# A graph kernel whose last three tiles of table rows are fetched one row at a time by the sync engine, with TensorE's turn put in another order

## The chip, the cores and the metric

The kernel runs on one core of a Trainium2 chip. A core has five engines that run side by side and meet only at semaphores: TensorE (PE), VectorE (DVE), ScalarE (ACT), GpSimd (POOL) and SyncE (SP), which here only issues DMA transfers. The metric is the device time of one launch in microseconds, as the median of several runs. One further execution was recorded by the profiler.

## The reference

Two graph layers over 3,125 nodes and 53,125 edges sorted by target, 128 features, all float32. Only the second one matters here:

```python
def sage_conv(x, src, dst, Wl, bl, Wr, n):      # layer 0, three of these with relu between
    agg = segment_sum(x[src], dst) / max(count, 1)
    return agg @ Wl.T + bl + x @ Wr.T

x = x + L0(relu(layernorm(x)), edges)
h = relu(layernorm(x))
messages = mlp(h[src] + edge_attr, We1, be1, We2, be2)   # gelu between the two products
aggregated = segment_sum(messages, dst)
x = x + mlp((1 + eps) * h + aggregated, Wu1, bu1, Wu2, bu2)
```

The kernel computes `h @ We1 + be1` once for each node and keeps it in HBM as `table` (3,125 rows of 512 bytes). For each edge it needs the row of its source node, added to `edge_attr @ We1`.

## The kernel before

The launch has a first part (adjacency counts and the three layers of L0, up to about 427 us), and then the **edge stage**, which the change touches. The edge stage walks over 416 tiles of 128 edges, in 105 groups `g` of 4 tiles (group 103 has three tiles, 412 to 414, and group 104 has one, 415). Each engine runs its own loop over turns `g`, written out by hand; what one engine hands to another is counted in a semaphore.

- **TensorE**, turn `g`: `mix(g + 2)` multiplies the edge attributes of a group by `We1` into one of three PSUM banks (`z_ready`); it waits for the edge load and for `pre_ready` of the group that had the bank. `take_sources` (line 1383) multiplies selection matrices for a picked group; `flip` (line 1392) transposes a picked group; `aggregate(g - 1)` (line 1425) adds the messages of a group to their nodes. The nodes come in seven chunks `c`; when the last group of a chunk is in, `node_mix`, `node_up` and `node_down` (lines 1400 to 1412) do the node MLP, with a turn for each set by `node_due`. Chunk 5 ends with group 100, chunk 6 with group 104.
- **GpSimd** fetches the source rows of a group from `table` by one indirect DMA for each tile (line 653) into a ring of six groups, `rows`. 15 of the 105 groups are "picked" (3, 10, 17, ..., 101): their rows come from TensorE's selections instead and are not gathered. That leaves 356 gathers.
- **VectorE**, turn `g`: the selection matrices of the picked groups (`select_sources`, line 945), the one-hot matrix of a group's targets (`window_onehots`, line 917), and then `pre = z + rows` (line 1061), which waits for `z_ready` and for the group's gathers. Ahead of them in a turn stand the sums of the node chunks (`node_sum`, line 959; chunk 5's in the turn of group 103).
- **ScalarE** applies GELU to `pre` (line 1205) to give `msg`, copies the flipped groups, copies a chunk's aggregate (line 1188) and applies the chunk's GELU (line 1191).
- **SP** issues the loads: `load_edges(u)` (line 509) brings the edge attributes of three groups (768 KB) into one of two buffers, once `z_ready` shows that the buffer is free; line 595 loads the source indices of a picked group, and line 598 stores a chunk. Its queue holds each instruction until the one before it is issued.

The first part also has a place that a prediction can use: line 1087, where ACT reads a value from SBUF into a register for each of 213 groups (`value_load`), checks its bounds, and computes an address.

Of the kernel before, what the change touches and what calls it, by code (L numbers as in the profile page):

```python
# [7 lines left out]
ALU = mybir.AluOpType  # L8
# [10 lines left out]
P = 128  # L19
# [209 lines left out]
def fast_path(nc, s, t, table, counts, inv, outT, spill):  # L229
# [21 lines left out]
    FLAG, KEEP = 12, 13  # L251
    with ExitStack() as ctx:
# [13 lines left out]
        def placed_at(name, shape, dt, offset):  # L266
# [51 lines left out]
        rows, o = carve(flat, 0, (RW, T * D), F32)  # L318
        pre, o = carve(flat, o, (PR, T * D), F32)
# [58 lines left out]
            sem("node_added"), sem("stored"))  # L378
        tile_in, dst_tile_in, abs_ready = sem("tile_in"), sem("dst_tile_in"), sem("abs_ready")
# [126 lines left out]
        def _(sp):  # L506
# [80 lines left out]
            sp.dma_start(order[0:EP, 1, :], t["dst_next"]).then_inc(order_in, 16)  # L587
            for g in range(END):
                if g % PER == PER - 1 and EA < g // PER + EA < UNITS:
                    sp.wait_ge(z_ready, g + 1)  # L590
                    load_edges(g // PER + EA)
                if g in s.picked and s.picked.index(g) + 2 < len(s.picked):
                    i = s.picked.index(g) + 2
                    sp.wait_ge(offset_ready, i - 1)
                    sp.dma_start(src_rows[:, i % 2, :], src_columns(i)).then_inc(src_in[i % 2], 16)
                for c in node_due(g, STORE):
                    sp.wait_ge(node_added, c + 1)
                    sp.dma_start(at(outT, c), at(xT, c)).then_inc(stored, 16)
# [3 lines left out]
        def _(pool):  # L602
# [43 lines left out]
            for g in range(G):  # L646
# [3 lines left out]
                for j in range(s.tiles(g)):  # L650
                    if j == 0 and r >= RW:
                        pool.wait_ge(pre_ready, r - RW + 1)
# [6 lines left out]
        def _(dve):  # L659
# [381 lines left out]
            for g in range(END):  # L1041
# [8 lines left out]
                if g < G:  # L1050
# [4 lines left out]
                    if g not in s.picked:  # L1055
                        r, w = s.by_rows(g), s.tiles(g) * D
                        dve.wait_ge(z_ready, g + 1)
                        dve.wait_ge(gathered[r % RW], 16 * sum(s.tiles(s.of_ordinal(q)) for q in range(r % RW, r + 1, RW)))
                        if r >= PR:
                            dve.wait_ge(msg_ready, s.of_ordinal(r - PR) + 1)  # L1060
                        dve.tensor_tensor(pre[:, r % PR, 0:w], z_group(g), rows[:, r % RW, 0:w],  # L1061
                                          ALU.add).then_inc(pre_ready, 1)
# [146 lines left out]
        def _(pe):  # L1209
# [222 lines left out]
            for g in range(END):  # L1432
                if g + AHEAD < G:
                    mix(g + AHEAD)
# [11 lines left out]
                for i, b in s.selections(g):  # L1446
                    take_sources(i, b)
                if g + 1 in s.picked:
                    flip(s.picked.index(g + 1))
                if 1 <= g <= G:  # L1450
                    aggregate(g - 1)
# [590 lines left out]
```

## Time and profile before

| | |
|---|---|
| median of 3 runs | 892.18 us (891.96 to 892.45) |
| profiled execution, its own time | 890.32 us |
| its span (first to last instruction) | 888.5 us |
| granted TensorE clock, mean | 0.983 of full speed |
| busy: PE, DVE, POOL, ACT | 814.7, 668.0, 389.2, 322.8 us |
| gathers of line 653 | 356, 337.4 us busy |
| selection matmuls of line 1383 | 750, 204.8 us busy |

Busy times are sums over the whole span; several engines overlap. A matmul's end is modelled, so a busy TensorE is not one at its peak. The profiled execution has a time of its own, 1.86 us under the median; differences are taken from its rows and then put to the median.

### The profile page before, as it was taken

How to read it: one execution, taken by the hardware profiler on the slowest of the kernel's cores; microseconds unless marked ns; L12 is line 12 of the kernel's file. 1: busy time of each engine (PE TensorE's matmuls, PEld its weight loads, DVE VectorE, ACT ScalarE, POOL GpSimd, SP SyncE). 2: the span in 40 equal slices, each digit the busy share in tenths (PEclk: the TensorE clock that was granted, in tenths of full speed). 3: DMA queues.
4: the chain of work that ended last, by engine and by line, in shares of the span. 5: the costliest groups of instructions: out<-in, count | busy, mean ns of one | idle time of the engine just before them, and what ended most of it. 6: DMA issues, size and time to landing. Idle time of an engine off the chain costs nothing.

```text
span 888.5 us, 14535 instructions
## 1 busy us (share of the span) xinstructions
PE 814.7 (92%) x4780; PEld 619.8 (70%) x4780; DVE 668.0 (75%) x1837; ACT 322.8 (36%) x568; POOL 389.2 (44%) x451
## 2 busy tenths in 40 slices
PE   3688999999999999999879999999899899989995
PEld 1244555555678887778668888887787797887883
DVE  8999999997254445454999878868876987686961
ACT  3576677775255555544111211121121111112211
POOL 1000000000022222322677777777777777777772
PEclk9999999999999999999989999999999999999997
DMA  4300011001000000010754444434334444433421
GB/s 111 119 1 13 3 14 14 13 2 25 1 1 1 1 1 12 24 48 24 143 183 134 138 122 136 128 122 148 117 109 147 122 123 128 137 114 109 137 78 35
DMA packets 37462, 67.51 MB, mean 76 GB/s; under 512 B 14825, under 2 KB 25028, under 8 KB 37124
## 3 DMA queue, kind: packets, MB, share of 16 engines
q1 hardware_dynamic: 25988, 43.16, 16.5%
q0 software_dynamic: 11392, 23.35, 9.8%
q8 instruction: 40, 0.66, 0.3%
q14 instruction: 42, 0.34, 0.2%
HBM read 63.18 MB, written 3.30 MB: 75 GB/s over the span
## 4 chain that ended last, share of the span: by engine, by line
PE 47%; DVE 22%; POOL 19%; issue 9%; DMA 1%; ACT 1%; POOLq 0%; SPq 0%; ACTq 0%; DVEq 0%
POOL f_adj L653 19%; PE f_ps L1328 15%; PE f_ps L1321 9%; DVE f_select L945 7%; PE f_ps L1383 4%; PE f_ps L1369 3%; PE f_ps L1226 3%; PE f_ps L1219 2%; PE f_ps L1425 2%; DVE f_adj L1061 2%; PE f_ps L1295 2%; DVE f_region L722 2%; DVE f_region L720 2%; DVE f_adj L917 2%; PE f_ps L1257 1%
## 5 line engine op out<-in xcount | busy, mean ns | idle before, releaser
L653 POOL DMA_INDIRECT f_adj<-table,f_by_edge x356 | 337.4, 948 | 109.4 <-issue 106.7
L945 DVE TENSOR_SCALAR f_select<-f_ps 128x512 fp32r<-128x512 f32 x375 | 234.1, 681 | 34.6 <-PE f_ps L1383 34.1
L1383 PE MATMUL f_ps<-f_select,f_pair 125*128 125x512 f32 x750 | 204.8, 419 | 3.0 <-DVE f_select L945 3.0
L638 POOL CAST f_wide<-f_adj 125x500 fp32r<-125x500 uint8 (+1 forms) x70 | 40.4, 577 | 357.8 <-ACT f_adj L1091 211.9
L1205 ACT ACTIVATE f_adj<-f_adj 128x512 f32<-128x512 f32 (+1 forms) x90 | 56.3, 625 | 336.7 <-DVE f_adj L1061 336.7
L1383 PEld LDWEIGHTS f_ps<-f_select,f_pair 125*128 125x128 f32 x750 | 139.6, 193 | 44.3 <-issue 11.5
L1328 PE MATMUL f_ps<-f_wide,f_pair 125*128 125x500 f32 (+1 forms) x700 | 162.5, 385 | 1.5 <-DVE f_wide L777 0.6
L1091 ACT CAST f_adj<-f_ps 128x500 f32 x213 | 125.9, 591 | 55.1 <-PE f_ps L1226 42.7
L1328 PEld LDWEIGHTS f_ps<-f_wide,f_pair 125*128 125x128 f32 x700 | 122.4, 189 | 33.4 <-issue 6.2
L1425 PEld LDWEIGHTS f_ps<-f_adj 128*128 128x128 f32 x984 | 124.0, 192 | 13.6 <-issue 6.8
L1425 PE MATMUL f_ps<-f_adj 128*128 128x94 f32 (+20 forms) x984 | 123.8, 271 | 4.8 <-ACT f_adj L1205 4.6
L1321 PE MATMUL f_ps<-f_adj,f_parts 125*128 125x500 fp8e4 (+1 forms) x525 | 127.9, 353 | 0.0
L1369 PE MATMUL f_ps<-f_We,f_region 128*128 128x128 f32 x688 | 97.5, 286 | 21.3 <-DVE f_adj L1061 21.3
L1369 PEld LDWEIGHTS f_ps<-f_We,f_region 128*128 128x128 f32 x688 | 85.3, 195 | 25.7 <-issue 25.7
L1138 ACT CAST f_wide<-f_adj 125x500 fp32r<-125x500 uint8 (+1 forms) x140 | 78.1, 565 | 60.5 <-PE f_ps L1328 59.7
L1061 DVE TENSOR_TENSOR f_adj<-f_ps,f_adj 128x512 f32<-128x512 f32 (+1 forms) x90 | 60.8, 676 | 49.7 <-issue 34.3
L777 DVE CAST f_wide<-f_adj 125x500 fp32r<-125x500 uint8 (+1 forms) x140 | 57.6, 421 | 52.9 <-PE f_ps L1328 52.6
L1219 PE MATMUL f_ps<-f_region 125*128 125x300 f16 (+1 forms) x213 | 67.0, 315 | 29.9 <-DVE f_region L726 24.3
L1226 PE MATMUL f_ps<-f_region 125*128 125x375 f16 x212 | 74.0, 349 | 0.0
L1219 PEld LDWEIGHTS f_ps<-f_region 125*128 125x128 f16 x213 | 20.9, 98 | 69.4 <-ACT f_adj L1091 32.9
L722 DVE TENSOR_SCALAR f_region<-f_iota,f_by_edge 125x375 f16<-125x375 f16 x212 | 67.1, 317 | 0.0
L720 DVE TENSOR_SCALAR f_region<-f_iota,f_by_edge 125x300 f16<-125x300 f16 x212 | 62.2, 293 | 4.1 <-PE f_ps L1226 3.7
(149 smaller groups left out, 695.3 us busy)
## 6 DMA issues: line engine op xcount, KB each, us to landing
f_region<-in_edge_attr_T SPq DMA_DIRECT2D x33, 768.0 KB
f_adj<-table,f_by_edge POOLq DMA_INDIRECT x356, 2.6
f_src_rows<-in_src_row SPq DMA_DIRECT2D x14, 256.0 KB, 4.8
f_xT<-in_xT SPq DMA_DIRECT2D x1, 1562.5 KB, 6.4
f_adj<-inv SPq DMA_DIRECT2D x1, 1562.5 KB, 7.0
out<-f_xT SPq DMA_DIRECT2D x6, 250.0 KB, 2.3
table<-f_region SPq DMA_DIRECT2D x6, 224.0 KB
f_rcntT<-inv SPq DMA_DIRECT2D x5, 250.0 KB, 3.8
```

The costliest lines, as they stand in the source:

```text
L653: pool.indirect_dma_start(out=rows[:, r % RW, j * D:(j + 1) * D], out_offset=None, in_=table, in_offset=bass.IndirectOffsetOnAxis(ap=table ...
L720: dve.tensor_scalar(keys[0:EP, slot, 0:s.A_COLS], iota[0:EP, 0:s.A_COLS], key[0:EP, tt:tt + 1], None, ALU.is_equal)
L722: dve.tensor_scalar(keys[0:EP, slot, s.A_COLS:KEYS], iota[0:EP, s.B_FROM:s.DW * NB], key[0:EP, tt + 1:tt + 2], None, ALU.is_equal)
L945: ins = dve.tensor_scalar(select[:, u % SELECT, :], offset, float(b * NP - CENTRE), None, ALU.is_equal)
L1091: act.copy(adj[:, :, bass.ds(base, s.DW)], ps[:, build_ps(g):build_ps(g) + s.DW * NB].rearrange("p (w b) -> p b w", b=NB)).then_inc(kept, 1)
L1219: pe.matmul(ps[:, o:o + wide], lows[0:EP, slot, 0, :], keys[0:EP, slot, 0:wide], start=True, stop=g == 0, skip_group_check=True)
L1226: ins = pe.matmul(ps[:, o + s.B_FROM:o + s.DW * NB], lows[0:EP, slot, 1, :], keys[0:EP, slot, s.A_COLS:KEYS], start=False, stop=True, skip ...
L1321: ins = pe.matmul(ps[:, dense_ps(i):dense_ps(i) + width(c)], parts1[0:NP, p, b, :], adj[0:NP, b, lo:hi].bitcast(F8), start=b == 0 and p == ...
L1328: ins = pe.matmul(ps[:, dense_ps(i):dense_ps(i) + streamed(c)], pair[l][0:NP, p, b, :], wide_tile(u), start=b == 0 and p == 0, stop=b == N ...
L1369: ins = pe.matmul(z_ps(g, j), edge_tiles(g, j, j + 1), weights["We1"][:, :], start=True, stop=True)
L1383: ins = pe.matmul(z_columns(g), chosen[0:NP, p, b, :], select[0:NP, u % SELECT, :], start=b == 0 and p == 0, stop=b == NB - 1 and p == 1, ...
L1425: ins = pe.matmul(agg_ps(c, lo, hi), msg[:, g % MS, j * D:(j + 1) * D], onehot[:, g % OH, j, at_lo:at_lo + hi - lo], start=opens and j == ...
```

## The change

The tiles 413, 414 and 415 leave GpSimd's list. SP fetches their 384 rows, four in each of its turns from turn 2 to turn 97: it reads the row's index from SBUF into a register, checks it, multiplies it to an address, and issues a DMA of one row (512 bytes) into a buffer of its own, `far`. VectorE's `pre` of group 103 waits for all 384 (`fetched`), and adds the one near tile and the two far ones by an instruction each; group 104 has a far tile only, and waits for no gather. TensorE's turn, which was `mix`, node chunks, selections, flip, aggregation, becomes node chunks, selections, `mix`, aggregation, flip.

```diff
--- before.py
+++ after.py
@@ -249,6 +249,10 @@
     TAKE, MIX, SUM, UP, ACTIVE, DOWN, ADD, STORE = 2, 3, 4, 4, 4, 5, 6, 8
     END = G + STORE + 1
     FLAG, KEEP = 12, 13
+    FAR = [s.FT - 1, s.FT - 2, s.FT - 3]
+    ROWS, FIRST_ROWS = 4, 2
+    FAR_GROUP = G - 2
+    NEAR = s.tiles(FAR_GROUP) - sum(s.tile(FAR_GROUP) <= q < s.tile(G - 1) for q in FAR)
     with ExitStack() as ctx:
         k = {}
 
@@ -316,6 +320,7 @@
         tmp, o = carve(early, o, (3, NT), F32)
 
         rows, o = carve(flat, 0, (RW, T * D), F32)
+        far, o = carve(flat, o, (len(FAR), D), F32)
         pre, o = carve(flat, o, (PR, T * D), F32)
         msg, o = carve(flat, o, (MS, T * D), F32)
         onehot, o = carve(flat, o, (OH, T, W), F32)
@@ -376,6 +381,7 @@
         node_mixed, node_summed, up_mixed, up_active, down_mixed, node_added, stored = (
             sem("node_mixed"), sem("node_summed"), sem("up_mixed"), sem("up_active"), sem("down_mixed"),
             sem("node_added"), sem("stored"))
+        fetched = sem("fetched")
         tile_in, dst_tile_in, abs_ready = sem("tile_in"), sem("dst_tile_in"), sem("abs_ready")
         order_in, checked, flagged, be2_ready = sem("order_in"), sem("checked"), sem("flagged"), sem("be2_ready")
         smooth, flipped = sem("smooth"), sem("flipped")
@@ -585,7 +591,16 @@
             sp.dma_start(rstdT[:, :], inv.partition_broadcast(P)).then_inc(rstd_in, 16)
             sp.dma_start(order[0:EP, 0, :], t["dst_rows"]).then_inc(order_in, 16)
             sp.dma_start(order[0:EP, 1, :], t["dst_next"]).then_inc(order_in, 16)
+            def fetch_row(n):
+                q, p = n // P, n % P
+                i = sp.value_load(table_idx[p:p + 1, FAR[q]:FAR[q] + 1], min_val=0, max_val=N - 1)
+                sp.dma_start(far[p:p + 1, q, :], table[bass.ds(i, 1), :]).then_inc(fetched, 16)
+
+            sp.wait_ge(tile_in, 32)
             for g in range(END):
+                if FIRST_ROWS <= g:
+                    for n in range((g - FIRST_ROWS) * ROWS, min(len(FAR) * P, (g - FIRST_ROWS + 1) * ROWS)):
+                        fetch_row(n)
                 if g % PER == PER - 1 and EA < g // PER + EA < UNITS:
                     sp.wait_ge(z_ready, g + 1)
                     load_edges(g // PER + EA)
@@ -648,6 +663,8 @@
                     continue
                 r = s.by_rows(g)
                 for j in range(s.tiles(g)):
+                    if s.tile(g) + j in FAR:
+                        continue
                     if j == 0 and r >= RW:
                         pool.wait_ge(pre_ready, r - RW + 1)
                     pool.indirect_dma_start(
@@ -1055,11 +1072,24 @@
                     if g not in s.picked:
                         r, w = s.by_rows(g), s.tiles(g) * D
                         dve.wait_ge(z_ready, g + 1)
-                        dve.wait_ge(gathered[r % RW], 16 * sum(s.tiles(s.of_ordinal(q)) for q in range(r % RW, r + 1, RW)))
+                        near = [s.tiles(s.of_ordinal(q)) for q in range(r % RW, r + 1, RW)]
+                        if g == FAR_GROUP:
+                            dve.wait_ge(fetched, 16 * P * len(FAR))
+                            near[-1] = NEAR
+                        if g < G - 1:
+                            dve.wait_ge(gathered[r % RW], 16 * sum(near))
                         if r >= PR:
                             dve.wait_ge(msg_ready, s.of_ordinal(r - PR) + 1)
-                        dve.tensor_tensor(pre[:, r % PR, 0:w], z_group(g), rows[:, r % RW, 0:w],
-                                          ALU.add).then_inc(pre_ready, 1)
+                        w, at_far = NEAR * D if g == FAR_GROUP else w, FAR.index(s.tile(g + 1) - 1) if g >= FAR_GROUP else 0
+                        if g < G - 1:
+                            ins = dve.tensor_tensor(pre[:, r % PR, 0:w], z_group(g)[:, 0:w], rows[:, r % RW, 0:w], ALU.add)
+                        else:
+                            ins = dve.tensor_tensor(pre[:, r % PR, 0:w], z_group(g), far[:, at_far, :], ALU.add)
+                        if g == FAR_GROUP:
+                            for j in range(NEAR, s.tiles(g)):
+                                ins = dve.tensor_tensor(pre[:, r % PR, j * D:(j + 1) * D], z_ps(g, j),
+                                                        far[:, FAR.index(s.tile(g) + j), :], ALU.add)
+                        ins.then_inc(pre_ready, 1)
                 if g == 0:
                     check_tiles()
                 if g == 1:
@@ -1430,8 +1460,6 @@
             for g in range(AHEAD):
                 mix(g)
             for g in range(END):
-                if g + AHEAD < G:
-                    mix(g + AHEAD)
                 if g == FLAG:
                     pe.wait_ge(flagged, 6)
                     pe.matmul(ps[0:1, FLAG_PS:FLAG_PS + 1], flag[:, 3:4], unit[:, 0:1],
@@ -1445,10 +1473,12 @@
                         node_down(c)
                 for i, b in s.selections(g):
                     take_sources(i, b)
+                if g + AHEAD < G:
+                    mix(g + AHEAD)
+                if 1 <= g <= G:
+                    aggregate(g - 1)
                 if g + 1 in s.picked:
                     flip(s.picked.index(g + 1))
-                if 1 <= g <= G:
-                    aggregate(g - 1)
                 for c in node_due(g, DOWN):
                     if c == NC - 2:
                         node_down(c)
```

How the instructions stand, as the built programs have it. On **SP**, where the edge stage begins (`f_adj<-inv` and the `in_dst` rows are the last loads ahead of its loop), before:

```order
L585 DMA f_adj<-inv 128x3125 [waits f_rstd_out]
L586 DMA f_adj<-in_dst_rows 125x425
L587 DMA f_adj<-in_dst_next 125x425
L595 DMA f_src_rows<-in_src_row 128x512 [waits f_offset_ready]
L509 DMA f_region<-in_edge_attr_T 128x1536 [waits f_z_ready] x2
```

SP had nothing to issue there but loads, each at a wait. After, in the same loop, at the end of turn 5 (`f_by_edge` holds the indices, the two `ISA` rows are register operations and an assert, the last is the address; `f_adj<-table` is one row):

```order
L597 DMA f_adj<-table 1x128
L515 DMA f_region<-in_edge_attr_T 128x1536 [waits f_z_ready]
L596 TENSOR_LOAD f_by_edge
L596 ISA x2
L597 ISA
L597 DMA f_adj<-table 1x128
```

The first edge load of the loop now has sixteen rows ahead of it, and twelve more stand between it and the next.

On **PE**, turns 99 and 100 (line 1383 are selections, 1425 aggregations of groups 98 and 99, 1369 `mix` of group 102, 1392 the flip of group 101), before:

```order
L1383 MATMUL f_ps<-f_select,f_pair_49 128x512
L1425 MATMUL f_ps<-f_adj 128x80 [waits f_msg_ready,f_oh_ready]
L1425 MATMUL f_ps<-f_adj 128x80 x3
L1425 MATMUL f_ps<-f_adj 128x14 [waits f_node_added]
L1425 MATMUL f_ps<-f_adj 128x14 x3
L1369 MATMUL f_ps<-f_We,f_region 128x128 [waits f_pre_ready,f_ea_in0]
L1369 MATMUL f_ps<-f_We,f_region 128x128 x3
L1392 MATMUL f_ps<-f_ident,f_flipping 128x128 [waits f_smooth]
L1392 MATMUL f_ps<-f_ident,f_flipping 128x128 x3
L1425 MATMUL f_ps<-f_adj 128x50 [waits f_msg_ready,f_oh_ready]
L1425 MATMUL f_ps<-f_adj 128x50 x3
L1425 MATMUL f_ps<-f_adj 128x44 x4
```

After, the same place (lines 1413, 1455, 1399, 1422, and 1395, the `mix` of the picked group 101):

```order
L1413 MATMUL f_ps<-f_select,f_pair_49 128x512
L1395 MATMUL f_ps<-f_region,f_We 128x512 [waits f_rows_kept,f_ea_in1]
L1455 MATMUL f_ps<-f_adj 128x80 [waits f_msg_ready,f_oh_ready]
L1455 MATMUL f_ps<-f_adj 128x80 x3
L1455 MATMUL f_ps<-f_adj 128x14 [waits f_node_added]
L1455 MATMUL f_ps<-f_adj 128x14 x3
L1399 MATMUL f_ps<-f_We,f_region 128x128 [waits f_pre_ready,f_ea_in0]
L1399 MATMUL f_ps<-f_We,f_region 128x128 x3
L1455 MATMUL f_ps<-f_adj 128x50 [waits f_msg_ready,f_oh_ready]
L1455 MATMUL f_ps<-f_adj 128x50 x3
L1455 MATMUL f_ps<-f_adj 128x44 x4
L1422 MATMUL f_ps<-f_ident,f_flipping 128x128 [waits f_smooth]
```

The flip has gone behind the aggregation of group 99, and the `mix` of group 101, which stood ahead of turn 99's selections, now stands behind them.

On **DVE**, the last groups (1061 is `pre` of 102, 103 and 104, 959 the sum of chunk 5, 963 its end), before:

```order
L1061 TENSOR_TENSOR f_adj<-f_ps,f_adj 128x512 [waits f_msg_ready,f_gathered3,f_z_ready]
L959 TENSOR_TENSOR f_rcntT<-f_rcntT,f_ps 128x500 [waits f_h_scaled,f_node_mixed]
L1061 TENSOR_TENSOR f_adj<-f_ps,f_adj 128x384 [waits f_msg_ready,f_gathered4,f_z_ready]
L1061 TENSOR_TENSOR f_adj<-f_ps,f_adj 128x128 [waits f_msg_ready,f_gathered5,f_z_ready]
L963 SCALAR_TENSOR_TENSOR f_xT<-f_ps,f_bu,f_xT 128x500 [waits f_down_mixed]
```

After (lines 1085, 1090 and 1087 are `pre`, 976 the sum of chunk 5):

```order
L1085 TENSOR_TENSOR f_adj<-f_ps,f_adj 128x512 [waits f_msg_ready,f_gathered3,f_z_ready]
L976 TENSOR_TENSOR f_rcntT<-f_rcntT,f_ps 128x500 [waits f_h_scaled,f_node_mixed]
L1085 TENSOR_TENSOR f_adj<-f_ps,f_adj 128x128 [waits f_gathered4,f_msg_ready,f_fetched,f_z_ready]
L1090 TENSOR_TENSOR f_adj<-f_ps,f_adj 128x128 x2
L1087 TENSOR_TENSOR f_adj<-f_ps,f_adj 128x128 [waits f_msg_ready,f_z_ready]
L980 SCALAR_TENSOR_TENSOR f_xT<-f_ps,f_bu,f_xT 128x500 [waits f_down_mixed]
```

The sum of chunk 5 still stands ahead of `pre` of group 103, which is now three additions, the first of which has the new wait; group 104 waits for no gather.

## Rows read from the trace of the kernel before

**Rows 1.** Line 653, POOL's gathers: ns min/median/max, first and last start; landing.

```profile
L653 POOL DMA_INDIRECT f_adj<-table,f_by_edge x356: 940/944/2035, 427.0 to 871.7; - x178
...
DMA to landing us min/median/max: 2.4/2.6/6.3
```

**Rows 2.** POOL's waits, line 653: us in total, times, longest.

```profile
POOL f_adj L653 <- issue: 106.7, 350, 0.3
POOL f_adj L653 <- DVE f_adj L1061: 1.5, 5, 0.3
```

**Rows 3.** DVE's waits, 450 to 870 us.

```profile
DVE f_adj L1061 <- issue: 34.3, 15, 4.9
```

**Rows 4.** PE's waits, 450 to 870 us.

```profile
PE f_ps L1369 <- DVE f_adj L1061: 21.3, 33, 1.9
```

**Rows 5.** Timeline of SP, 440 to 452 us: start, us, engine, line.

```profile
443.19 0.35 SPq L587 DMA_DIRECT2D f_adj<-in_dst_next  x1
443.59 0.36 SPq L595 DMA_DIRECT2D f_src_rows<-in_src_row  x1
```

**Rows 6.** Line 509, SP's edge loads, as in group 1.

```profile
L509 SPq DMA_DIRECT2D f_region<-in_edge_attr_T x34: 327/328/432, 426.7 to 844.6; - x34
```

**Rows 7.** Lines 1087 and 1091 (ACT's queue) and 516 (SP's), as in group 1.

```profile
L1087 ACTq TENSOR_LOAD <-f_first x213: 272/278/482, 4.6 to 214.1; - x107
L1087 ACTq FUSED_REGOPS  x213: 147/147/166, 5.1 to 214.5; - x107
L1087 ACTq SEQ_ASSERT  x213: 18/18/29, 5.3 to 214.6; - x107
...
L1091 ACTq ALU_OP  x213: 35/35/43, 9.7 to 214.8; - x107
...
L516 SPq DMA_DIRECT2D f_first<-in_tile_first x1: 299/299/299, 2.3 to 2.3; - x1
```

**Rows 8.** DMA view: one edge load, KB and median us to landing.

```profile
f_rcntT<-in_edge_attr_T SPq DMA_DIRECT2D x1, 768.0 KB, 4.7
```

**Rows 9.** Timeline of the tail: start us, us, engine, line, operation [idle before <-releaser].

```profile
861.70 1.14 PE L1369 MATMUL f_ps<-f_We,f_region 128*128 128x128 f32 x8
...
867.93 0.94 POOL L653 DMA_INDIRECT f_adj<-table,f_by_edge  x1 [0.30 <-issue]
...
870.88 0.67 DVE L959 TENSOR_TENSOR f_rcntT<-f_rcntT,f_ps 128x500 f32<-128x500 f32 x1 [0.91 <-PE f_ps L1402]
...
871.77 1.04 PE L1408 MATMUL f_ps<-f_rcntT,f_Wu 128*128 128x500 f32 x2
...
872.94 0.56 DVE L1061 TENSOR_TENSOR f_adj<-f_ps,f_adj 128x384 f32<-128x384 f32 x1 [1.38 <-DMA f_adj<-table,f_by_edge]
...
873.59 0.52 ACT L1205 ACTIVATE f_adj<-f_adj 128x384 f32<-128x384 f32 x1 [2.90 <-DVE f_adj L1061]
...
874.14 0.29 DVE L1061 TENSOR_TENSOR f_adj<-f_ps,f_adj 128x128 f32<-128x128 f32 x1 [0.64 <-ACT f_adj L1205]
...
874.26 1.14 PE L1425 MATMUL f_ps<-f_adj 128*128 128x54 f32 x8 [1.45 <-ACT f_adj L1205]
...
874.58 0.30 ACT L1205 ACTIVATE f_adj<-f_adj 128x128 f32<-128x128 f32 x1
...
875.24 1.53 PE L1412 MATMUL f_ps<-f_hT,f_Wu 128*128 128x500 f32 x2
...
877.88 0.79 PE L1408 MATMUL f_ps<-f_rcntT,f_Wu 128*128 128x125 f32 x2 [0.38 <-DVE f_rcntT L959]
```

**Rows 10.** Windows of the tail; PEclk is the number ahead of the DMA share.

```profile
870.00:872.00 2.00, 2.00 (x13) 1.39 (x12) 0.67 (x1) 0.63 (x1) 1.39 (x3) 1.00 0.13 33
...
876.00:878.00 2.00, 1.62 (x7) 0.80 (x6) 1.02 (x2) 0.00 (x0) 0.00 (x0) 0.50 0.00 0
```

**Rows 11.** Line 1992, one value load on each engine at the end.

```profile
L1992 SPq TENSOR_LOAD <-spill x1: 482/482/482, 883.5 to 883.5; - x1
L1992 ACTq TENSOR_LOAD <-spill x1: 280/280/280, 883.5 to 883.5; - x1
```

## The prediction

> **What bounds the kernel now.** I read the gathers of the edge stage first, since the change takes three of them away. In the view of their source line the reader is to see 356 indirect gathers from 427.0 to 871.7, half of the whole span [rows 1]. The waits of POOL say what stands between them: 0.3 us of its own issue, 350 times, and DVE only 5 times, for the same 0.3 us [rows 2]. So nothing ever holds POOL back: (871.7 - 427.0) / 355 gives one gather every 1.253 us, an unbroken chain. DVE's waits ahead of the `pre` addition are the other side: 15 waits, up to 4.9 us, put down to "issue" because the gather that it waits for ended long before its data landed [rows 3]. Fifteen is the number of picked groups; once in each cycle of seven groups DVE has caught up with POOL. TensorE and VectorE therefore run behind POOL by a few microseconds and recover, and POOL's chain sets when the stage ends. TensorE still waits 21.3 us in 33 waits for `pre` at the head of its turn [rows 4]; that is what the second edit is about.
>
> After the last gather comes a tail: `pre` of group 103 at 872.94, aggregation to 875.40, the node chain, the last store [rows 9].
>
> **Part 1: three gathers off POOL.** They are the last three, so every group up to 102 gets its rows when it did before. The last gather is now tile 412, at 867.93 [rows 9] in place of 871.7 [rows 1]: three gathers of 1.25, 3.75 us on POOL. How much of it reaches the end is read from the tail. Tile 412 lands 2.6 us after issue (the median [rows 1]), at 870.5. But DVE has the node sum of chunk 5 ahead of it, 870.88 to 871.55 [rows 9], and that hangs on group 100, which the change doesn't touch. So `pre` of 103 starts at 871.55 at the earliest, in three additions of one tile in place of one of three: 3 x 0.29, where 0.29 is the one-tile addition of group 104 [rows 9], bring it to 872.42, where before it ended at 873.50. ACT then has GELU of 103, GELU of chunk 5 (which waits for TensorE's matmul of 871.77 + 1.04 = 872.81 [rows 9]) and GELU of 104. Before, the first and the last of these started 873.59 and 874.58, 0.99 apart. Started at 872.5, they put the last at 873.5: 1.1 us earlier. TensorE's aggregation of 104, chunk 5's and chunk 6's node chains follow, all queued behind these. **Gain: 1.1 us**, and not 3.75.
>
> There is a second, smaller piece. TensorE is granted its full clock in 870 to 872 and half of it (1.2 GHz in place of 2.4) in 876 to 878 [rows 10]; between them it sat idle from 872.81 to 874.26, waiting for group 103. With 103 ready at about 873, that hole shrinks to a few tenths. What it costs now: the two 500-column passes of 875.24 take 1.53 us, the same shape at 871.77 took 1.04 [rows 9]. That is 0.5 us, and the 125-column pairs behind it (0.79 us each at the low clock [rows 9]) may give back some 0.3 us each, my estimate from that same ratio. Whether the clock stays up no row can tell; bounds 0 and 1.4 us, I take 0.9. **Sum of part 1: 2.0 us.**
>
> **Part 2: 384 rows on SP.** Each costs SP five instructions ahead of the next. The rows of before show four of the five kinds, on ACT for the register side: the load of a value 278 ns, its fused register operations 147, the assert 18 (medians of 213 [rows 7]); a DMA of one partition on SP 299 ns [rows 7]. The second fused pair (two multiplications, to the byte address) isn't shown; it lies between one plain register operation, 35 ns, and the fused three, 147 [rows 7]. I take two thirds of the latter, 98. Between instructions SP shows 443.19 + 0.35 to 443.59, some 0.04 us [rows 5]; five such are 0.2, or 0.15 if the register kinds follow closer. Sum: 0.278 + 0.147 + 0.018 + 0.098 + 0.299 + 0.18 = **1.02 us a row**. Lower bound, with 35 ns and the narrow gaps: 0.93. Upper: no DMA whose address comes from a register is in the trace; the dearest plain load issue on SP is 0.432 [rows 6], with which, 147 ns and the wide gaps a row is 1.22.
>
> What SP can afford: it enters the loop at 443.54 [rows 5]. Its last edge load (groups 102 to 104, issued at 844.6 before [rows 6]) is now behind all the rows. The matmuls that read it start at 861.70 [rows 9]; a transfer of that size lands 4.7 us after issue [rows 8], so it must be issued by 857.0. From these 413.5 us go 32 loads, 13 source-row loads and 5 stores at 0.33 + 0.04, 18.5 us: 395 us for 384 rows, **1.029 us a row**. Under that the work is hidden: SP only waited for `z_ready` there. Above it every 0.01 us on a row costs 384 x 0.01 = 3.8 us, since TensorE waits for the loads queued behind the rows and everything waits for TensorE. 1.02 against 1.029 is nearly no margin, and this is the whole risk of the change.
>
> The additional bytes (384 x 512 B) are nothing against the 768 KB of one edge load [rows 8]. POOL's issue doesn't slow: its median gather is within 4 ns of its shortest while loads run beside it all the time [rows 1]. DVE's new wait for all 384 rows stands at group 103, some 13 us after the latest issue that the loads allow, so it is never last.
>
> **Part 3: TensorE's order.** Selections no longer queue behind a `mix` that waits for `pre`, so part of the 21.3 us [rows 4] goes; the flip no longer holds up an aggregation. `mix` comes later in its turn, by five selections at most, but its result is read two turns later. Since POOL is never held [rows 2], TensorE's time is worth nothing here: **0**, bounds 0 and a gain of 0.3 x 5 = 1.5, if DVE's five releases [rows 2] were true waits, which their 0.3 us, no longer than POOL's own issue, excludes. From turn 101 on the two orders are the same. The cover is POOL's chain; if SP becomes the bound, the reorder does not help either, since the loads are late.
>
> Sum: 0.9 + 1.1 = 2.0 off the profiled 890.32, or off the median 892.18, which stands 1.86 above it: **890.2**.
>
> **Rivals.**
> *SP can't keep up.* A row costs more than 1.029 us. For it: the register-addressed DMA is unseen, and the margin is 0.01. Against: medians from 213 repetitions, and the same cost on both queues wherever both show one. At 1.06 us it gives 890.2 + 0.031 x 384 = 902; at 1.10, 917; it decides from 1.035 on, where the gain is used up.
> *Reads on SP stay dear.* SP's only value load took 482 ns, in the place where ACT's took 280 [rows 11]. Against: ACT's own first took 482 too and its median is 278 [rows 7], so the first read is dear and not the engine. If it stayed, 0.2 us more a row: 890.2 + (1.22 - 1.029) x 384 = 964. The Trainium skill's page "DMA: Bandwidth & Descriptors", section "Latency and other measured facts", speaks for this one, and against the change: it gives a register load (`tensor_load`) a floor of about 600 ns. By it a row would be 1.34 us and the time about 1010; 213 loads at 278 ns contradict it here.
> *All of it comes back.* If chunk 5's chain is not in the way (its sum runs in a hole), the end moves by the 3.75 us of POOL: 888.4. Against: the node sum stands ahead of `pre` in DVE's order.
>
> **Numbers.** Forecast 0.55; SP can't keep up 0.33; dear reads 0.04; all of it 0.08. The forecast's own range is 888.6 to 891.5. Range for 8 in 10: 888.0, a little past the third rival, to 903, which is a row of 1.06 us; what is dearer is left out. About 0.2% (1.8 us) is what can be told from no change. The forecast lies on that edge: 0.31 faster, 0.23 same, 0.01 slower; SP can't keep up: 0.04 same, 0.29 slower; dear reads slower; all of it faster. Together 0.39, 0.27, 0.34.
>
> **What would show it.** Right: SP's row at or under 1.02 us from load to load, gathers every 1.25 us, last gather at 868, edge loads issued in time, the last aggregation about 1.1 us earlier, the clock at full after 875. Wrong: TensorE waiting for the edge load at `mix`, POOL waiting for `pre`, turns longer than the 4.2 us of now (105 in the 444.7 us of [rows 1]), SP never waiting for `z_ready`.

## The result and the profile after

The changed kernel took **981.21 us** (978.36 to 982.26) against 892.07 before on the same chip: a ratio of 1.0999, with a 95% interval of 1.0983 to 1.1015. It is 89 us slower; 890.2 was forecast, and the range ended at 903. The profiled execution took 978.36 us, with a span of 976.4 and a mean granted clock of 0.923 of full speed.

Lines 596 and 597 hold SP's row fetch, the answer to [rows 7]: ns min/median/max, first and last start.

```profile
L596 SPq TENSOR_LOAD <-f_by_edge x384: 434/497/674, 444.0 to 946.5; - x192
L596 SPq FUSED_REGOPS  x384: 147/152/176, 444.5 to 947.0; - x192
L596 SPq SEQ_ASSERT  x384: 18/18/37, 444.8 to 947.2; - x192
...
L597 SPq FUSED_REGOPS  x384: 37/37/48, 444.8 to 947.3; - x192
L597 SPq MOVE f_adj<-table x384: 29/29/38, 444.9 to 947.3; - x192
L597 SPq DMA_DIRECT2D f_adj<-table x384: 254/258/290, 445.0 to 947.4; - x192
```

The reads run from 444.0 to 946.5, and the prediction needed the last rows before 857. Less the 18.5 us that the prediction counts for the other instructions of SP, a row takes (946.5 - 444.0 - 18.5) / 383 = 1.264 us, where the limit was 1.029. The six medians add up to 0.991 us, and the read alone is half of them.

Who waits for SP then is seen in the waits of 450 to 960 us (total, times, longest):

```profile
DVE f_select L962 <- PE f_ps L1413: 146.0, 40, 12.7
...
POOL f_adj L670 <- DVE f_adj L1085: 74.8, 20, 9.1
PE f_ps L1399 <- DMA f_region<-in_edge_attr_T: 71.8, 22, 8.0
```

The same waits before, over 450 to 870 us, have no row in which TensorE waits for an edge load, POOL's waits for DVE are those of [rows 2], and DVE's for the selections were

```profile
DVE f_select L945 <- PE f_ps L1383: 34.1, 42, 2.8
```

SP's own waits for an edge buffer over the whole span, after and before:

```profile
SPq L515 <- PE f_ps L1399: 0.9, 3, 0.4
```

```profile
SPq L509 <- PE f_ps L1369: 314.1, 28, 17.2
```

TensorE's `mix` waits for an edge load in 22 of its turns, up to 8.0 us, since the load stands behind rows in SP's queue. DVE waits for TensorE, and POOL, which nothing held before, for DVE. SP itself hardly waits for a free buffer any more. It is the bound, and the chain that ended last has 30% of the span on SP's queue.

The tail, as in [rows 9], has the shape that was forecast, 90 us later (start, us, engine, line):

```profile
961.30 0.68 DVE L976 TENSOR_TENSOR f_rcntT<-f_rcntT,f_ps 128x500 f32<-128x500 f32 x1 [4.70 <-PE f_ps L1432]
961.89 0.28 DVE L1085 TENSOR_TENSOR f_adj<-f_ps,f_adj 128x128 f32<-128x128 f32 x1
...
963.33 1.24 PE L1455 MATMUL f_ps<-f_adj 128*128 128x54 f32 x8 [0.20 <-ACT f_adj L1235]
...
964.41 1.08 PE L1442 MATMUL f_ps<-f_hT,f_Wu 128*128 128x500 f32 x2
...
967.46 0.49 PE L1442 MATMUL f_ps<-f_hT,f_Wu 128*128 128x125 f32 x2 [0.46 <-ACT f_hT L1221]
```

`pre` of group 103 starts right behind the node sum of chunk 5. The hole ahead of the last aggregation is 0.20 us, where it was 1.45; the two 500-column passes take 1.08 in place of 1.53, and the 125-column pair 0.49, where [rows 9] has 0.79 for such a pair. From the node sum to the end of the span it is 976.4 - 961.30 = 15.1 us; before, 888.5 - 870.88 = 17.6 [rows 9].

That alone doesn't show a gain from the three gathers, since two kernels below in which GpSimd still fetches every tile have the same short tail. In `e1_order` the node sum of chunk 5 starts at 874.53 of a span of 889.8, 15.3 us before its end, and in `e7_actreads` at 874.68 of 889.9, 15.2 us. `e1_order`, then `e7_actreads`:

```profile
874.53 0.67 DVE L959 TENSOR_TENSOR f_rcntT<-f_rcntT,f_ps 128x500 f32<-128x500 f32 x1 [2.12 <-PE f_ps L1402]
```

```profile
874.68 0.67 DVE L959 TENSOR_TENSOR f_rcntT<-f_rcntT,f_ps 128x500 f32<-128x500 f32 x1 [3.30 <-PE f_ps L1407]
...
876.59 1.37 PE L1430 MATMUL f_ps<-f_adj 128*128 128x54 f32 x8
...
877.79 1.08 PE L1417 MATMUL f_ps<-f_hT,f_Wu 128*128 128x500 f32 x2
```

There is no hole ahead of the last aggregation of `e7_actreads`, and its 500-column passes take 1.08 us too. The profiled execution of before is the one whose node sum came early, at 870.88, and which then waited for the last gathers.

### The profile page after: what moved, and what is told of

Same layout as the page of the kernel before. It is cut to its first block, busy times and chain, and to the rows that moved or that the text cites. A ratio compares the mean times of both kernels' runs of the same rounds, so it can differ in the third digit from the quotient of the medians.

```text
span 976.4 us, 16839 instructions
## 1 busy us (share of the span) xinstructions
PE 850.3 (87%) x4780; PEld 655.0 (67%) x4780; DVE 667.5 (68%) x1839; ACT 322.9 (33%) x568; POOL 388.4 (40%) x448
## 4 chain that ended last, share of the span: by engine, by line
PE 45%; SPq 30%; DVE 9%; issue 9%; DMA 5%; ACT 1%; ACTq 0%; DVEq 0%
SPq L596 19%; PE f_ps L1358 14%; SPq L597 9%; PE f_ps L1351 9%; PE f_ps L1413 5%; PE f_ps L1455 4%; PE f_ps L1399 3%; DMA f_region<-in_edge_attr_T 3%; PE f_ps L1256 3%; PE f_ps L1249 2%; PE f_ps L1325 2%; DVE f_region L739 2%; DMA inv<-f_rstd 2%; DVE f_region L737 1%; PE f_ps L1287 1%
## 5 line engine op out<-in xcount | busy, mean ns | idle before, releaser
L1413 PE MATMUL f_ps<-f_select,f_pair 125*128 125x512 f32 x750 | 212.0, 433 | 6.6 <-DVE f_select L962 6.6
L1413 PEld LDWEIGHTS f_ps<-f_select,f_pair 125*128 125x128 f32 x750 | 150.3, 208 | 41.7 <-issue 8.8
L1399 PE MATMUL f_ps<-f_We,f_region 128*128 128x128 f32 x688 | 108.5, 308 | 71.8 <-DMA f_region<-in_edge_attr_T 71.8
L1399 PEld LDWEIGHTS f_ps<-f_We,f_region 128*128 128x128 f32 x688 | 100.7, 218 | 84.7 <-DMA f_region<-in_edge_attr_T 79.8
L1455 PEld LDWEIGHTS f_ps<-f_adj 128*128 128x128 f32 x984 | 137.1, 216 | 8.4 <-issue 7.9
L1455 PE MATMUL f_ps<-f_adj 128*128 128x94 f32 (+20 forms) x984 | 140.3, 294 | 0.2 <-ACT f_adj L1235 0.2
L1351 PEld LDWEIGHTS f_ps<-f_adj,f_parts 125*128 125x128 bf16 x525 | 47.4, 97 | 25.1 <-issue 1.7
```

The lines of the kernel that those rows point to most:

```text
L1351: ins = pe.matmul(ps[:, dense_ps(i):dense_ps(i) + width(c)], parts1[0:NP, p, b, :], adj[0:NP, b, lo:hi].bitcast(F8), start=b == 0 and p == ...
L1399: ins = pe.matmul(z_ps(g, j), edge_tiles(g, j, j + 1), weights["We1"][:, :], start=True, stop=True)
L1413: ins = pe.matmul(z_columns(g), chosen[0:NP, p, b, :], select[0:NP, u % SELECT, :], start=b == 0 and p == 0, stop=b == NB - 1 and p == 1, ...
L1455: ins = pe.matmul(agg_ps(c, lo, hi), msg[:, g % MS, j * D:(j + 1) * D], onehot[:, g % OH, j, at_lo:at_lo + hi - lo], start=opens and j == ...
```

## The experiments

What had to be told apart: is the loss SP's own time, or is it the 384 transfers, or the new order of TensorE's turn? And if it is SP's time, why is a read 497 ns there when ACT's was 278 [rows 7]? Rivals for that: the engine, the place of the data (other partitions of SBUF, a loaded stage), or the neighbour in the queue: a read is slow only behind a DMA issue (B, where an expectation uses letters). Each diff shows the main part of its edit; definitions, loops and waits that were adapted to it are left out.

**1. Addresses without reads.** `e3_noread` fetches as many rows, but from fixed addresses, so its far rows aren't those of the indices.

```diff
-                i = sp.value_load(table_idx[p:p + 1, FAR[q]:FAR[q] + 1], min_val=0, max_val=N - 1)
-                sp.dma_start(far[p:p + 1, q, :], table[bass.ds(i, 1), :]).then_inc(fetched, 16)
+                sp.dma_start(far[p:p + 1, q, :], table[n:n + 1, :]).then_inc(fetched, 16)
```

> The changed kernel with its 384 one-row DMAs, but at fixed addresses: no index is read, checked or multiplied, so the rows are those of the wrong nodes. If SP's own time is the whole loss, a row costs SP the DMA alone (0.258 us and the gap, 0.30), SP waits for z_ready again, and what is left is the gain in the tail that the prediction worked out, 2.0 us: about 890. If the 384 small transfers themselves disturb the edge loads or the gathers, it stays well above 892 (910 or more).

Measured: 891.58 us, ratio 1.0005 (0.9995 to 1.0015). SP's waits in its trace:

```profile
SPq L515 <- PE f_ps L1398: 231.2, 28, 15.8
...
SPq L515 <- PE f_ps L1394: 33.4, 4, 11.0
```

The 384 transfers stay and the whole loss goes. SP waits for buffers again, 265 us in all. So it is SP's own time. But the 2.0 us that the prediction expected from the tail don't show in the time either; experiments 6 to 9 are about that.

**2. Reads without row DMAs.** `e4_readonly` reads and checks all 384 values and doesn't use them; three plain DMAs of 128 fixed rows stand for the 384.

```diff
-                i = sp.value_load(table_idx[p:p + 1, FAR[q]:FAR[q] + 1], min_val=0, max_val=N - 1)
-                sp.dma_start(far[p:p + 1, q, :], table[bass.ds(i, 1), :]).then_inc(fetched, 16)
+                sp.value_load(table_idx[p:p + 1, FAR[q]:FAR[q] + 1], min_val=0, max_val=N - 1)
+                if p == P - 1:
+                    sp.dma_start(far[:, q, :], table[q * P:(q + 1) * P, :]).then_inc(fetched, 16)
```

> The changed kernel with the 384 reads and checks on SP, but no DMA behind them: one DMA for each of the three tiles brings 128 rows at fixed addresses (the rows of the wrong nodes). Theory A, SP's sequencer reads slowly whatever stands ahead: a read stays at 0.48 to 0.50 us. Theory B, a read is slow because a DMA issue stands ahead of it: here, behind another read, it falls to ACT's 0.28. In both a row costs under 0.8 us, SP keeps up, and the time is about 890.

Measured: 889.57 us in a single run. Its reads:

```profile
L596 SPq TENSOR_LOAD <-f_by_edge x384: 260/270/1010, 444.1 to 838.3; - x192
```

The same engine, the same data and the same stage: 270 ns. What is gone from between the reads is the row DMA with its address arithmetic.

Not every DMA issue makes the next read dear, though. The loads and stores at fixed addresses still stand among these reads. From 445 to 503 us SP issues six loads, each directly ahead of a read:

```profile
448.83 0.36 SPq L611 DMA_DIRECT2D f_src_rows<-in_src_row  x1
453.65 15.99 SPq L515 DMA_DIRECT2D f_region<-in_edge_attr_T  x2
474.09 0.33 SPq L611 DMA_DIRECT2D f_src_rows<-in_src_row  x1
479.25 11.84 SPq L515 DMA_DIRECT2D f_region<-in_edge_attr_T  x2
```

and no read of that stretch takes over 286 ns:

```profile
L596 SPq TENSOR_LOAD <-f_by_edge x63: 262/270/286, 445.0 to 497.2; - x63
```

Of the 44 reads of the stage that stand directly behind such a load or store, 42 take 264 to 279 ns. The other two took 462 and 463. The second of them is the first read after one of this kernel's plain DMAs of table rows, and the first read after another of these took 462 too (the third has none behind it). So it may be a DMA from the table that matters, and not the address in a register; two reads are too few to say.

**3. The same reads on ACT**, unused, in the kernel before.

```diff
+                if 2 <= g:
+                    for n in range((g - 2) * 4, min(3 * P, (g - 1) * 4)):
+                        act.value_load(table_idx[n % P:n % P + 1, s.FT - 1 - n // P:s.FT - n // P], min_val=0,
+                                       max_val=N - 1)
```

> The kernel before with the same 384 reads and checks added to ACT, four in each turn from turn 2; nothing uses them. Theory A (the engine): 0.28 us a read, as ACT's 213 earlier ones. Theory C (the place: an index in another partition each time, while loads and gathers fill the memory): 0.45 to 0.50 on ACT too. ACT is busy for a sixth of this stage, so the time stays within 10 us of before.

Measured: 891.85 us in a single run, beside 890.83 for before.

```profile
L1187 ACTq TENSOR_LOAD <-f_by_edge x384: 272/282/583, 447.1 to 854.2; - x192
```

282 ns for these words in this stage: the place of the data isn't it.

**4. Four reads, then four DMAs.** The same instructions in each of SP's turns, in another order.

```diff
-                i = sp.value_load(table_idx[p:p + 1, FAR[q]:FAR[q] + 1], min_val=0, max_val=N - 1)
-                sp.dma_start(far[p:p + 1, q, :], table[bass.ds(i, 1), :]).then_inc(fetched, 16)
+                i = [sp.value_load(table_idx[p:p + 1, FAR[q]:FAR[q] + 1], min_val=0, max_val=N - 1) for q, p in at]
+                for (q, p), i in zip(at, i):
+                    sp.dma_start(far[p:p + 1, q, :], table[bass.ds(i, 1), :]).then_inc(fetched, 16)
```

> The changed kernel with the four reads of a turn first and its four DMAs behind them; same instructions. Theory A (the engine): all reads at 0.50, a row still 1.26 us, about 979. Theory B (the DMA ahead): one read in four at 0.50, the others at 0.28, a row at 1.10 us, by 3.8 us for each 0.01 above 1.029 about 915.

Measured: 904.34 us in a single run, 77 us less than the changed kernel.

```profile
L596 SPq TENSOR_LOAD <-f_by_edge x384: 260/273/902, 444.4 to 868.7; - x192
...
L598 SPq DMA_DIRECT2D f_adj<-table x384: 224/228/301, 447.1 to 870.7; - x192
```

The median read is 273 ns: three of four stand behind another read's check, and only the first of a turn behind a DMA. This is the theory of the neighbour, which had 1.10 us a row and about 915 us; a row costs (868.7 - 444.4 - 18.5) / 383 = 1.06 us, and the DMAs, now behind one another, 228 ns in place of 258 are a part of the difference. That is still above the limit, and the prediction's first rival had 902 us for just that row.

**5. The check between the DMA and the next read.** The value is read a row ahead, so that its check (152 + 18 ns) stands between a row's DMA and the next read. Instructions and their number are those of the changed kernel.

```diff
-                i = sp.value_load(table_idx[p:p + 1, FAR[q]:FAR[q] + 1], min_val=0, max_val=N - 1)
+                i = nc.s_assert_within(ahead.pop() if n else read(0), 0, N - 1)
+                if n + 1 < len(FAR) * P:
+                    ahead.append(read(n + 1))
                 sp.dma_start(far[p:p + 1, q, :], table[bass.ds(i, 1), :]).then_inc(fetched, 16)
```

> The changed kernel with the same 1,920 register instructions, reads and row DMAs in another order: the check of a value (152 + 18 ns) now stands between a row's DMA and the next row's read, so the read is no longer directly behind a DMA. Theory one (the queue is still at work for a while behind a DMA's issue, and the read waits out what is left): the read falls by about the 170 to 200 ns of the check, to some 300 ns, the row to 1.06 us, the time to 900 to 905 us, as with the four reads together. Theory two (a read that has a DMA issue ahead of it since the last read costs 500 ns, wherever it stands): the read stays at some 500 ns and the time at 977 to 983 us.

Measured: 957.67 us in a single run, which is neither.

```profile
L596 SPq TENSOR_LOAD <-f_by_edge x384: 274/436/762, 444.3 to 924.5; - x192
```

The check gives the read 61 ns back (497 to 436), not the 170 to 200 that a queue busy for a while behind its DMA would give. More time doesn't help either. In `e9_both` (experiment 7) SP waits for free buffers, and 18 first reads of a turn start 1.5 to 9.5 us after the last row DMA was issued; their median is 462 ns. One of them, with the last row issued by 726.4 and an edge load at fixed addresses directly ahead:

```profile
721.38 5.04 SPq L599 DMA_DIRECT2D f_adj<-table  x8
733.51 0.37 SPq L515 DMA_DIRECT2D f_region<-in_edge_attr_T  x1
```

```profile
L596 SPq TENSOR_LOAD <-f_by_edge x1: 467/467/467, 733.9 to 733.9; - x1
```

So the first read after a row DMA is dear whenever it comes, by 166 to 192 ns over 270 (436 and 462), and directly behind the DMA by 227 in the changed kernel (497); the reads that follow it are at 270 again. A queue still at work can't be the cause of most of it, and neither can any DMA issue as such (experiment 2). What it is about the row DMA, its source, its shape or its address from a register, is not shown by these runs. The time fits, though: a row is (924.5 - 444.3 - 18.5) / 383 = 1.206 us, and 890.2 + (1.206 - 1.029) x 384 = 958.

**6. Below the limit: no check of the value** (`e6_unchecked`), and **7. both** (four reads together, no check: `e9_both`).

```diff
-                i = sp.value_load(table_idx[p:p + 1, FAR[q]:FAR[q] + 1], min_val=0, max_val=N - 1)
+                i = nc.values_load(table_idx[p:p + 1, FAR[q]:FAR[q] + 1], engines=(mybir.EngineType.SP,), min_val=0,
+                                   max_val=N - 1, skip_runtime_bounds_check_because="src is drawn from 0 to N - 1")
```

> The changed kernel with the check of the read value (the fused pair of 152 ns and the assert of 18 ns) left out; the values read are the same. The read still stands behind a DMA issue, so it should stay at some 500 ns, and a row at 1.26 - 0.17 for the two instructions and up to 0.07 of gaps between them = 1.02 to 1.09 us, at the limit of 1.029. Theory (slope of 384 us per us of row above the limit): 888 to 892 us at 1.02, 912 us at 1.09; in any case 65 us or more below the changed kernel. Rival (SP's rows load the DMA queues or the memory, and the time follows the count of transfers, not SP's own time): about 981 us again.

> The four reads of a turn together, then the four DMAs, and no check of the values. Row = 1.062 of the kernel with the four reads together, less 0.17 to 0.24 = 0.82 to 0.89 us, below the limit of 1.029: SP has 50 to 80 us to spare in the stage and should wait for z_ready again. Theory: within 0.2% of before or the tail's 2.0 us below it, 888.5 to 892 us. Rival (one-row DMAs cost the rest of the kernel even when SP keeps up): above 893 us.

Measured: 891.47 us, 1.0004 (0.9994 to 1.0014), and 891.78 us, 1.0007 (0.9997 to 1.0016). The first one's reads:

```profile
L596 SPq TENSOR_LOAD <-f_by_edge x384: 433/501/677, 444.9 to 847.9; - x192
```

Each read is as dear as in the changed kernel, 501 ns, but the row, (847.9 - 444.9 - 18.5) / 383 = 1.00 us, is under the limit, and 90 us are gone. `e9_both` has time to spare and gains nothing from it.

**8. Two tiles in place of three** (`e8_two`): the reads as they are, three rows in a turn.

```diff
-    FAR = [s.FT - 1, s.FT - 2, s.FT - 3]
-    ROWS, FIRST_ROWS = 4, 2
+    FAR = [s.FT - 1, s.FT - 2]
+    ROWS, FIRST_ROWS = 3, 2
```

> The changed kernel with two tiles on SP in place of three, three rows in a turn, the reads as they are (about 500 ns, a row at 1.26 us). 256 rows take 323 us of the 395 that SP has to give. Theory (the loss is only what SP's queue lacks): no loss of that kind, 890 to 893 us, with the order's 1.8 us in it. Rival (every slow read or row costs something, kept up or not): in proportion, 2/3 of 89 us, 950 us.

Measured: 892.25 us, 0.9997 (0.9988 to 1.0006). 256 rows at the full price fit, so a slow read costs nothing by itself.

**9. The order of TensorE's turn**, alone (`e1_order`), undone in the changed kernel (`e2_far`), and undone in `e9_both` (`e10_old_order`). The edit of the first is the last part of the change's diff; that of the other two is its reverse.

> The kernel before with the new order of TensorE's turn alone; every table row still comes by GpSimd's gathers. My theory (the reorder is worth nothing): within 0.2% of before, 889 to 893 us. The rival, that the order carries part of what happened, gives a time further from before than that: if TensorE's turn was what the gathers and VectorE waited for, below 889; if selections first delay the aggregates, above 893.

> The changed kernel with the old order of TensorE's turn: mix after the aggregate, the flip ahead of it as before. If SP's rows alone make the loss: 978 to 983 us, as the changed kernel. If the new order has a part in the 89 us, it comes out below 975 or above 986.

> The four reads together and unchecked, as in the run before, but with the old order of TensorE's turn. The order alone cost 1.8 us (0.7 to 2.8), and the rows on SP with the new order came out 0.6 us above before; so, if the two add up, the rows alone are worth 1.2 us (0 to 2.5): 888.8 to 891.3 us, and the granted clock should stay at 1.00 from 860 to 872 us as in before. Rival (the tail's gain doesn't exist, the order's cost and it are one and the same): within 0.5 us of before.

The expectation of `e2_far` puts `mix` behind the aggregation; its edit puts it at the head of the turn, as the kernel before has it. Measured: 892.31 us, 1.0020 (1.0008 to 1.0032); 984.02 in a single run, a little above its 978 to 983; 891.23, 0.9985 (0.9975 to 0.9995). With `e9_both` that fills a table:

| ratio to before | old order | new order |
|---|---|---|
| all gathers on POOL | 1 | 1.0020 |
| three tiles on SP, which keeps up | 0.9985 | 1.0007 |

The rows on SP are worth 0.13 to 0.15%, 1.2 to 1.3 us, in either order, and the new order costs 0.20 to 0.22%, 1.8 to 2.0 us, in either row. Each ratio is good to about 0.1% either way, so the worth of the rows stands outside its error only with the old order, while the order's cost does in both rows. It accounts for most of the 2.0 us missing in experiment 1. `e10_old_order` beats the kernel before by a little, with an interval that leaves out 1, and the changed kernel by far.

What the new order does is seen on TensorE. With it, in `e9_both`:

```profile
863.81 0.83 PE L1400 MATMUL f_ps<-f_We,f_region 128*128 128x128 f32 x6
866.54 1.98 PE L1456 MATMUL f_ps<-f_adj 128*128 128x20 f32 x16 [1.90 <-ACT f_adj L1236]
868.36 0.43 PE L1400 MATMUL f_ps<-f_We,f_region 128*128 128x128 f32 x2
868.62 1.79 PE L1456 MATMUL f_ps<-f_adj 128*128 128x95 f32 x8
870.20 1.93 PE L1431 MATMUL f_ps<-f_adj,f_We 128*128 128x500 f32 x2
```

and with the old one, in `e10_old_order`:

```profile
867.94 0.91 PE L1400 MATMUL f_ps<-f_We,f_region 128*128 128x128 f32 x6
868.69 1.91 PE L1456 MATMUL f_ps<-f_adj 128*128 128x20 f32 x16
870.43 0.43 PE L1400 MATMUL f_ps<-f_We,f_region 128*128 128x128 f32 x2
870.70 1.03 PE L1456 MATMUL f_ps<-f_adj 128*128 128x95 f32 x8
871.56 1.03 PE L1431 MATMUL f_ps<-f_adj,f_We 128*128 128x500 f32 x2
```

With the new order TensorE gets ahead, stands idle for 1.90 us ahead of the 20-column aggregations, and then runs the matmuls of chunk 5's end at half its clock (1.2 in place of 2.4 GHz): 1.79 and 1.93 us for what takes 1.03. The windows of the two (length, then PE's busy time; PEclk is the number ahead of the DMA share):

```profile
868.00:870.00 2.00, 2.00 (x15) 2.00 (x14) 0.09 (x1) 0.58 (x1) 1.27 (x2) 0.68 0.13 39
870.00:872.00 2.00, 2.00 (x5) 0.82 (x5) 0.60 (x1) 0.63 (x1) 0.00 (x0) 0.50 0.14 33
```

```profile
860.00:868.00 8.00, 8.00 (x58) 7.11 (x57) 2.75 (x6) 2.96 (x5) 5.91 (x7) 1.00 0.21 52
868.00:872.00 4.00, 4.00 (x34) 3.79 (x34) 0.89 (x2) 1.21 (x2) 1.89 (x2) 1.00 0.20 49
```

All six kernels with the new order in which POOL sets the pace (experiments 1, 2, 6 to 8 and `e1_order`) have a two-microsecond window at 0.50 to 0.57 between 868 and 874; before, `e7_actreads`, `e10_old_order` and `e11_inside` keep 1.00 from 864 to 874. It isn't the profiled executions alone: over twelve runs each, the mean granted clock of five of the six (experiment 2 has a single run) is 0.966 to 0.971, and that of `e10_old_order`, `e11_inside` and the runs of before beside them 0.976 to 0.980. From the start of the 20-column aggregations to the node sum it is 866.54 to 872.86 in `e9_both`, 6.3 us, and 868.69 to 873.26, 4.6 us, in `e10_old_order`. The difference, 1.7 us, has the size of the order's price. But in these two executions TensorE reaches the place 2.15 us earlier with the new order, so that its sum still comes 0.4 us before the other, and its profiled time is the shorter one, 889.93 against 890.18: that execution is the fastest of the twelve of `e9_both`. So these traces don't hold the price. The table gives it, and the clock as its cause is argued, not shown.

**10. Three tiles further in.** `e11_inside` is `e10_old_order` with the far tiles at the ends of groups 98, 99 and 100, the last of which closes chunk 5.

```diff
-    FAR = [s.FT - 1, s.FT - 2, s.FT - 3]
+    FAR_GROUPS = [g for g in range(G - 1) if g not in s.picked and s.tiles(g) == T][-4:-1]
+    FAR = [s.tile(g + 1) - 1 for g in FAR_GROUPS]
```

> As the run above, with the three tiles that SP fetches taken from the ends of groups 98, 99 and 100, ahead of the group with which chunk 5 closes, in place of the last three. GpSimd's last gather then starts 3 x 1.25 = 3.75 us earlier, and so does all that follows it, chunk 5's sum too. Theory (GpSimd's gathers set the end): 3 to 3.75 us below before, 887 to 888.5 us. Rival (TensorE, busy 94% of the stage, sets the end from there): no better than the run above by more than 0.5 us.

Measured: 891.26 us, 0.9985 (0.9977 to 0.9994), as `e10_old_order` and as the rival had it, not the 887 to 888.5 of the theory. Its windows:

```profile
860.00:868.00 8.00, 8.00 (x58) 7.11 (x57) 3.58 (x10) 2.96 (x5) 6.17 (x7) 1.00 0.21 55
868.00:872.00 4.00, 4.00 (x37) 4.00 (x37) 0.80 (x2) 0.82 (x2) 2.35 (x3) 1.00 0.20 57
872.00:874.00 2.00, 2.00 (x12) 1.20 (x11) 0.19 (x1) 0.28 (x1) 0.00 (x0) 1.00 0.00 0
```

TensorE is busy for every microsecond from 860 to 874. POOL's three gathers are saved ahead of chunk 5's end, and TensorE can't use them. So it isn't POOL's chain alone that sets the end of the stage, as the prediction has it.

## Why the prediction was wrong, step by step

- **The step that failed** is in part 2: "the load of a value 278 ns". It took 497. ACT's 213 reads [rows 7] have no DMA between them; in SP's row each read is the first after a row DMA. Experiments 2 and 3 show that neither the engine nor the place makes the difference, experiments 2, 4 and 5 that a row DMA since the last read does, however long ago, where a load or a store alone does not. Why it does stays open.
- **The other terms of the row** were near or on the dear side: second fused operations 37 for 98 (and a MOVE of 29 that wasn't counted), DMA 258 for 299, first fused operations 152 for 147. Without the read the instructions came to 0.494 us, where 0.562 was forecast; the gaps took 0.27 in place of 0.18. The row was 1.26 us, past the upper bound of 1.22, which had the read at 278 too.
- **The limit of 1.029 us and the slope of 384 us for each us of row** held. Rows of 1.06, 1.206 and 1.264 us give 902, 958 and 980 by them; 904.3, 957.7 and 981.2 were measured. Since a row's time is itself taken from the first and the last read, this says that the end follows the last read by about the same time in all three; the test of the limit is on its other side: at 1.00 (experiment 6) there is no loss.
- **Part 1, the tail.** The shape came, a small hole and the clock at full, but `e1_order` and `e7_actreads` have it with all the gathers on GpSimd, so 17.6 to 15.1 us can't be put down to the three gathers. The forecast took its 2.0 us from one execution in which chunk 5's sum came at 870.88; it comes at 872.77 to 876.27 in the nine other traces in which SP keeps up, and TensorE, busy from 860 on in `e10_old_order`, is what holds it there. What is shown is a net gain of 1.3 us (0.4 to 2.2) with the old order; by which path is open, and that it lies near the 2.0 is in part luck.
- **Part 3, the order at 0**, was wrong by a cost of 1.8 us (0.7 to 2.9). "Since POOL is never held [rows 2], TensorE's time is worth nothing here" left out what lies behind POOL: TensorE has its share in the last turns (experiment 10), and there an idle time of 1.9 us went with half the clock in the traces, which may be the price but isn't shown to be. Next to SP's loss it hardly counts: with the old order `e2_far` took 984.
- **The rivals.** "Reads on SP stay dear" had the read's price (482) and, by 0.2 us more a row, 964 us; it got a chance of 0.04 since ACT's first read was dear as well. It was the right case for a reason that it didn't give. That the first rival's "same cost on both queues wherever both show one" doesn't hold could be read from [rows 11], 482 ns on SP beside 280 on ACT. "SP can't keep up" had the mechanism behind it and the right price for each 0.01 us.
- The Trainium skill's page "DMA: Bandwidth & Descriptors", section "Latency and other measured facts", gives a register load a floor of about 600 ns. No median here reaches that (270, 282, 497), and the 1010 us that the prediction worked out from it were not measured; but it warned in the right direction, and the prediction set it aside on rows in which no DMA stood between the reads.
- **What would show it** named the signs that came: TensorE waiting for edge loads at `mix`, POOL waiting for `pre`, SP hardly waiting for a buffer.

## What to carry to other kernels

Take the price of a queue instruction from a row where it has the same neighbours, not from the same operation elsewhere; if there is none, the range must hold the dearest single row (here 482 ns on the very engine). When a queue is filled to 99% of what it can give, a forecast is a bet on its unit price: put reads together and DMAs together, leave out a check that isn't needed, or move fewer rows. An engine that is "off the path" on average can be the bound of the last turns. And before a difference between two traces is put down to a change, search for it in traces of kernels without the change: the short tail was there too.

## What was not expected of the hardware

- A read of a value from SBUF into a register of SP takes 270 ns behind another read's check and behind the issue of a load or a store at fixed addresses (experiment 2), 497 directly behind a row DMA, 436 with a check of 170 ns between the two, and still 462 when the last row DMA was issued 1.5 to 9.5 us ago (experiment 5).
- A one-row DMA with its address from a register is issued in 258 ns where each has a read ahead of it, and in 228 where most stand behind another of their kind (experiment 4); one with a fixed address takes 252 (experiment 1).
- TensorE's granted clock fell to 0.50 to 0.57 within or soon after an idle time of 1.9 to 2.2 us in the six kernels named in experiment 9; the four with the old order had no idle time of that length there, and kept 1.00.
